# The second half of the last softmax-sum addition of a pair, on VectorE instead of GpSimd

## The reference

```
layer 0:  K, Q, V = 1x1 convolutions of x;  M = K V^T per head;  Out = M^T Q
          x = batchnorm(conv1x1(Out, Wo) + x)
layer 1:  xn = group_norm(x, 32 groups);  q, k, v = split(w_qkv @ xn + b_qkv)   # 8 heads of 64 channels
          weight = softmax(q^T k / 8)                  # 1024 x 1024 per head, over the keys
          a = weight @ v;  out = x + w_proj @ a + b_proj
```

## Time and profile before

| what | value |
|---|---|
| median of 3 runs | 2539.09 us (2537.21 to 2540.24) |
| the profiled execution | 2540.45 us |
| its span | 2537.3 us |
| TensorE busy | 2466.6 us, 97% |
| VectorE busy | 1728.9 us, 68% |
| GpSimd busy | 1234.4 us, 49% |
| ScalarE busy | 1161.3 us, 46% |
| granted TensorE clock, mean | 0.991 |

### The profile page before, as it was taken

The page is one execution under the profiler, slowest core; times in us unless marked ns, Lnnn a source line. Parts: engine busy times, 40 slices in busy tenths (PEclk is TensorE's granted clock), DMA queues, the critical chain, the costliest instruction groups (busy, mean ns, idle before and its releaser), DMA issues.

```text
span 2537.3 us, 37438 instructions
## 1 busy us (share of the span) xinstructions
PE 2466.6 (97%) x12980; PEld 1618.3 (64%) x12980; DVE 1728.9 (68%) x2226; ACT 1161.3 (46%) x1499; POOL 1234.4 (49%) x621
## 2 busy tenths in 40 slices
PE   7999999999799999999999999999999999999987
PEld 6887888878555575557556655755565565557544
DVE  6455554546568866885787588578857866885776
ACT  3332232322355535654555455355555645553553
POOL 3330000000066746774766567377656756771762
PEclk9999999999899999999999999999999999999999
DMA  5431111013221141114022220502230241202001
GB/s 191 141 108 50 50 66 66 33 50 116 88 79 50 76 183 50 83 49 176 26 100 104 104 108 17 207 26 83 92 133 26 100 169 56 84 30 104 17 17 67
DMA packets 64185, 214.15 MB, mean 84 GB/s; under 512 B 9152, under 2 KB 9152, under 8 KB 63168
## 3 DMA queue, kind: packets, MB, share of 16 engines
q1 hardware_dynamic: 49504, 159.41, 17.1%
q0 software_dynamic: 14560, 52.96, 5.7%
HBM read 141.05 MB, written 71.30 MB: 84 GB/s over the span
## 4 chain that ended last, share of the span: by engine, by line
PE 82%; issue 8%; POOL 4%; DVE 3%; ACT 2%; POOLq 0%; ACTq 0%; DVEq 0%
PE psum L1258 16%; PE psum L1445 14%; PE psum L1507 14%; PE psum L1489 11%; PE psum L1277 7%; PE psum L1456 5%; POOL a_all L566 4%; PE psum L1301 4%; PE psum L1329 3%; PE psum L1521 3%; PE psum L1375 1%; ACT a_all L783 1%; PE psum L1269 1%; PE psum L1543 1%; PE psum L1389 1%
## 5 line engine op out<-in xcount | busy, mean ns | idle before, releaser
L566 POOL TENSOR_TENSOR a_all<-a_all 128x1024 f32<-128x1024 f32 x441 | 1059.9, 2403 | 500.2 <-ACT a_all L783 462.4
L783 ACT ACTIVATE a_all<-psum 128x1024 f32<-128x1024 f32 x512 | 496.6, 1022 | 65.8 <-PE psum L1489 51.9
L1507 PE MATMUL psum<-a_all 128*64 128x512 f32 x2048 | 495.7, 605 | 0.0
L1069 DVE TENSOR_REDUCE small<-psum 128x2 f32<-128x1024 f32 x326 | 399.7, 1226 | 125.6 <-PE psum L1456 123.1
L1258 PE MATMUL psum<-r_all 128*128 128x512 f32 x1920 | 455.8, 396 | 6.9 <-DVE r_all L1148 5.8
L1489 PE MATMUL psum<-r_all 64*128 64x512 f32 x3200 | 423.6, 395 | 4.5 <-ACT a_all L783 2.3
L1258 PEld LDWEIGHTS psum<-r_all 128*128 128x128 f32 x1920 | 360.4, 190 | 103.1 <-DVE r_all L922 10.2
L1445 PE MATMUL psum<-r_all 128*128 128x512 f32 x1536 | 372.2, 399 | 5.5 <-DVE r_all L1166 5.5
L1489 PEld LDWEIGHTS psum<-r_all 64*128 64x128 f32 x3200 | 295.5, 185 | 92.1 <-ACT a_all L783 35.6
L1445 PEld LDWEIGHTS psum<-r_all 128*128 128x128 f32 x1536 | 284.4, 189 | 104.2 <-issue 42.9
L1507 PEld LDWEIGHTS psum<-a_all 128*64 128x64 f32 x2048 | 124.0, 136 | 235.2 <-issue 170.7
(11 more groups left out here) (144 smaller groups left out, 2495.5 us busy)
## 6 DMA issues: line engine op xcount, KB each, us to landing
r_all<-w_dram SPq DMA_DIRECT2D x48, 1024.0 KB, 4.9
xn_dram<-a_all POOLq DMA_DIRECT2D x56, 512.0 KB, 5.4
r_all<-xn_dram SPq DMA_DIRECT2D x7, 4096.0 KB, 15.4
a_all<-y_dram SPq DMA_DIRECT2D x9, 2048.0 KB, 8.6
a_all<-x SPq DMA_DIRECT2D x16, 1024.0 KB, 6.4
y_dram<-a_all SPq DMA_DIRECT2D x16, 1024.0 KB, 4.2
out<-a_all SPq DMA_DIRECT2D x32, 512.0 KB, 4.0
w_dram<-a_all POOLq DMA_DIRECT2D x16, 512.0 KB, 3.0
```

The source lines that it names most:

```text
L566: pool.tensor_tensor(p_sum[:, :, cols], probs[:, 0, :, cols] if i == 1 else p_sum[:, :, cols], probs[:, i % SLOTS, :, cols], ALU.add).then ...
L783: act.activation(probs[:, i % SLOTS, :, cols], psum[half][:, :, :], ACT.Exp, scale=SCALE).then_inc(probs_ready, 1)
L1069: dve.reduce_max(max2[:, :, tile, half], psum[3][:, :, :], AX_X).then_inc(work_free, 2)
L1507: last = pe.matmul(psum[2][h * D:(h + 1) * D, half], v_t[:, i, head], probs[:, i % SLOTS, h, half * HALF:(half + 1) * HALF], start=(i == 0 ...
```

## The change

In every pair but the very last, GpSimd leaves out the addition of tile 7, second half. VectorE makes it in `end_add`, directly behind `max_join`, and counts it in a new semaphore `end_added`. It waits for the last exponential of the pair and for GpSimd's 12th addition (tile 6, second half). ADDS is 13 now. Who waited for the 14th addition waits for `end_added` as well or instead: TensorE ahead of the sums, and ScalarE ahead of writing the slot again. The load of the residual now waits for the sums' matmuls (`sums_full`) instead of `sum_step` and `pv_done`.

```
-        ADDS = 2 * (NT - 1)
+        ADDS = 2 * (NT - 1) - 1
 # SyncE, ahead of the residual's load
-                sp.wait_ge(pv_done, ONE + (b + 1) * PAIRS * NT)
                 if last:
+                    sp.wait_ge(pv_done, ONE + (b + 1) * PAIRS * NT)
                     sp.wait_ge(sum_step, LAST_SUMS + NT - 1)
                     sp.wait_ge(last_sums, NT - 1)
                 else:
-                    sp.wait_ge(sum_step, ONE + (b + 1) * PAIRS * ADDS)
+                    sp.wait_ge(sums_full, ONE + (b + 1) * PAIRS)
 # GpSimd
-                        for half in range(1 if last_pair else NH):
+                        for half in range(1 if last_pair or i == NT - 1 else NH):
 # ScalarE, first exponentials of a batch, and of the pairs behind it
                                     act.wait_ge(sum_step, ONE + pairs * ADDS)
+                                    act.wait_ge(end_added, ONE + pairs)
...
-                                act.wait_ge(sum_step, ONE + (pairs - 1) * ADDS + 2 * (before - 1) + half + 1)
+                                if before == NT - 1 and half == 1:
+                                    act.wait_ge(end_added, ONE + pairs)
+                                else:
+                                    act.wait_ge(sum_step, ONE + (pairs - 1) * ADDS + 2 * (before - 1) + half + 1)
 # VectorE
+            def end_add(pairs):
+
+                cols = slice(HALF, N)
+                dve.wait_ge(probs_ready, ONE + (pairs + 1) * 2 * NT)
+                dve.wait_ge(sum_step, ONE + pairs * ADDS + ADDS - 1)
+                dve.tensor_tensor(p_sum[:, :, cols], p_sum[:, :, cols], probs[:, (NT - 1) % SLOTS, :, cols],
+                                  ALU.add).then_inc(end_added, 1)
...
                         max_join(NH + (pairs + 1) * len(COPIED))
+                        end_add(pairs)
 # TensorE, ahead of the sums
                     pe.wait_ge(sum_step, ONE + (pairs + 1) * ADDS)
+                    pe.wait_ge(end_added, ONE + pairs + 1)
```

More of the change, by code:

```diff
@@ L243, in build @@
         last_sums = sem("last_sums")
+        end_added = sem("end_added")
         o_ready = sem("o_ready")
@@ L1152, in _ @@
             dve.sem_inc(hid_lo_done, HID0)
+            dve.sem_inc(end_added, ONE)
             dve.sem_inc(max_reduced, NH)
```

## The result

The changed kernel takes 2521.88 us (median of 4 runs, 2521.16 to 2522.81) against 2539.66 us before (4 runs): 17.8 us less, ratio 0.9932 with a 95% interval of [0.9915, 0.9949]. The same kernel timed again on two more chips gave 16.8 us less (2522.84 against 2539.67) and 18.6 us less (2522.88 against 2541.43). The profiled execution took 2522.81 us for a span of 2521.3.

What follows compares the result with a forecast made beforehand. TensorE was taken as the bound, waiting 22.0 us for GpSimd ahead of the sums in 8 places. 9.2 + 2.5 + 2.2 - 1.5 = 12.4 us less gave 2526.8 us (chance 0.50), range 2522.5 to 2537.

Steps and rivals of the forecast that it cites:

- Parts 1 to 3: Additions: GpSimd saves 2.46 us per pair; VectorE enters the lock first, GpSimd ends at T+3.50; 23 transitions inside batches gain 0.
- T: End of GpSimd's 12th addition in a pair (tile 6, second half), which releases VectorE's addition and GpSimd's 13th.
- Part 4: Ends of batches 0 to 5: TensorE's 1.93 us wait vanishes, less 0.4 us handed on; worth 9.2 us.
- I charge 0.4 us: At each end of batches 0 to 5, value tile 2's copy ends about 1598.5, TensorE wants its bank at 1598.2.
- Part 6: One more wait ahead of each of 31 sums, charged 0.05 us each: 1.5 us lost.
- up to 1.4 us back; I take 0: Sums ahead of the last pair: a shorter wait may cost TensorE less clock, up to 1.4 us; counted as 0.
- Part 5: End of batch 6 gains 2.5 us, the last transition ahead of the last pair 2.2 us.
- (d): Rival, whole kernel: no wait costs anything and the clock stays up; 15.3 us less, 2523.8 us; chance 0.07.
- (a): Rival, the lock: GpSimd gets in first, delaying max_rows inside batches; 4.7 us less, 2534.4 us; chance 0.22.
- (b): Rival, batch ends: value banks or L704 come 1.5 us later, six gains vanish; 3.2 less, 2535.9 us; chance 0.13.
- (c): Rival, transitions inside batches: GpSimd first, max_rows' 0.85 us lateness reaches TensorE in all 23; slower, 2548 us; chance 0.08.

Runs made afterwards that it cites:

- the waits alone: Kernel before, with VectorE only counting in end_added and TensorE waiting for it ahead of 31 sums, GpSimd keeping 14 additions: 2538.46 us against 2539.67, ratio 0.9998.
- the other pairs alone: Changed kernel with the addition moved only in the first three pairs of every batch (24 additions): 2538.42 us against 2540.77 for the kernel before.
- the batch ends alone: Changed kernel with the addition moved only in the fourth pair of batches 0 to 6 (7 additions): 2530.13 us against 2540.77 for the kernel before.

## Why the prediction was right and wrong

**Parts 1 to 3 held.** T and the order at the lock: VectorE's addition started 0.03 us behind T in batches 0 to 5 and 0.10 behind it in the last two (0.07 was forecast), and took 1.23 us in all 31 pairs. GpSimd's run of 13 was forecast at "about 33 us" and is 32.89 to 32.95 in batches 0 to 5. L1054 was forecast 1.4 us sooner; it now lasts 0.79 us instead of 2.30. Transitions within a batch were forecast to be worth 0: 45.83 us in both, and the kernel with only these and the last transition confirms it (1374.76 against 1375.03 us for six batches).

**Part 4, the first step that failed, by its size.** All of the 1.93 us went at the batch ends, as said. "I charge 0.4 us" did not come: batches 1 to 5 are 1.87 to 1.94 us shorter. ScalarE's chain ended 4.87 us behind the start of the sums (1589.65 - 1584.78), where the prediction had 5.26 us (1596.1 - 1590.84); it had added up single durations, and in the trace after, instructions of one engine that follow each other overlap by about 0.1 us (L717 starts at 1585.17, twice 0.72 us would end at 1586.61, and L659 starts at 1586.41). The copy of tile 2 ended at 1591.99, and TensorE wanted the bank at 1586.64 + 2 x 2.75 = 1592.13. It was met by 0.14 us, where 0.3 us too late was worked out. The 9.2 us should have been 11.4: the term of 0.4 us per batch end was mis-sized; it measures 0.0 to 0.1.

**Part 6, the second step that failed.** 1.5 us were charged for 31 waits; the run with the waits alone shows none, by its batches of the same length.

**The third, a term that was missing.** The wait of 1.93 us costs more than itself: at one of the six batch ends the clock fell behind it in each profile of a kernel that has it, 1.5 us. The prediction put nothing for the clock there, without a reason. It considered this only at the 7.80 us wait, where "up to 1.4 us back; I take 0" was right at the sums: the clock was 0.50 behind the shorter wait too (2447.20 to 2451.00), and the sums took 3.68 us against 3.35.

**Part 5.** Batch 6 gave 1.95 us and not 2.5. Its end had a wait of 2.65, now 0.42, so 2.2 came, and 0.3 went between its first two sums, 46.03 us (2131.01 to 2177.04) against 45.69 before. ScalarE shows a wait of 2.1 us with no releaser there (ahead of 2142.51), but that is hardly the cause: with the other pairs alone the stretch takes 45.98 us and has no such wait, and with the addition left out it takes 45.84 and has one of 1.9. The cause stays open. At the last transition the wait fell by 1.70 us and the stretch up to it by 1.74, not by 2.2: GpSimd's 13 additions took 33.88 us there where 29.94 + 3.50 = 33.44 was reckoned. That 2.4 us came all the same, with the 0.64 of the stretch behind, is luck: from these sums to the last ones it took 0.35 us more than before (36.87 against 36.52), and behind the last sums 1.0 us less (37.13 against 38.12), where the change touches nothing; why was not followed.

Together: 12.4 + 2.2 + 1.5 + 1.5 - 0.55 + 0.2 = 17.25 us, between the 16.8 and 18.6 us that three chips gave. The two charges and the missing term were small, and all had the same sign. The range reached down to 2522.5; its rival (d), 2523.8, gave back the waits and the clock ahead of the last pair, kept the 0.4 us at each batch end and had nothing for the clock there.

**The rivals.** (a) did not happen, and the run that forces it shows that its price was wrong as well: 13.8 us less than before, not 4.7. Its 0.4 us in 15 transitions was an addition of lateness that the chain swallowed. (b) did not happen: TensorE shows no wait for a copy of a value tile, and the bank of tile 0 was free 0.30 us ahead (1586.34 against 1586.64). (c) falls with (a), and where GpSimd was made to go first the transitions stayed at 45.84 us. (d) came nearest, and half of it held: the waits cost nothing, but the clock did not stay up (0.50).

## What to carry to other kernels

Moving work to an idle engine pays where the slow engine's last piece is what the bound engine waits for; the seven batch ends gave nearly all of this gain, 24 other moved additions about 2 us. Before giving a small charge to each hand-over, look whether durations laid end to end overlap in the trace, and whether several such charges all point one way. A short wait of TensorE can be priced above its length when the clock's rows show a fall behind one like it. And a difference of 1 or 2 us between two profiles is read stage by stage first: the clock, or an engine that stands with no releaser, can hide or feign it.

## What the runs showed of the hardware

The clock can fall behind a TensorE wait of only 1.93 us. In the four profiles of kernels with that wait (1.83 to 1.93 us) it does so at one of the six ends of batches 0 to 5, and not at the same one: batch 0 in the kernel before and in the one with the waits alone (230.50 and 230.51 us for the batch), batch 1 in the one with the other pairs alone (965.97 to 1196.47, 230.50 us), batch 3 in the one with the residual's load alone (1419.12 to 1649.62, 230.50 us). The kernel with the other pairs alone shows it a second time, behind the 2.69 us wait at the end of batch 6 (230.89 us for the batch, the clock 0.72 from 2285 to 2291). The other batches up to 5 with the same wait lack it, and in none of the nine profiles of kernels without that wait does a batch up to 5 show it. How often it comes in executions without a profile is not known.

The Trainium skill (page "SBUF — State Buffer", section "SBUF: two separate sides") says that whoever starts first keeps the shared port pair. The trace agrees: GpSimd's addition that started 0.04 us behind VectorE's took 3.45 us instead of 2.39. Here two engines released by one event went the same way 31 times out of 31, VectorE first: it started 0.03 to 0.10 us behind the event, GpSimd 0.08 to 0.14.

In batches 6 and 7, which are written out behind the hardware loop, an engine can stand for 2 to 3 us with no releaser. All nine profiles of kernels that moved the fourth pair's addition show ScalarE doing so for 1.9 to 2.2 us at the same exponential of batch 6, and the four others do not; the 3.15 us of VectorE are in the run with the batch ends alone. The waits followed up here end 1.5 to 1.8 us behind the start of an 8 KB `instruction` packet (2141.00 and 2142.51 in the changed kernel, 2140.01 and 2141.53, 2164.64 and 2166.38 in the run with the batch ends alone). That loading of code is the cause is a guess from these times; other such packets have no wait beside them, and no run tested it.
